# Layer 0 of a four-layer graph network: the two operands of the edge-counting matmuls change places

## The reference

```python
m = relu(node_feat[src] + edge_feat)                      # 200000 x 32
neigh = segment_sum(m, dst, num_segments=N)               # by destination
x = layernorm(x + (1.0 + eps[0]) * node_feat + neigh)
```

## Time and profile before

| | us |
|---|---|
| median of 3 runs | 11489.69 |
| lowest and highest of them | 11487.98, 11491.17 |
| the profiled execution, first to last instruction (its span; the profile gives no other time of it) | 11493.4 |
| layer 0's loop in it, first pick to last | 169.4 to 1386.3 |

### The profile page before, as it was taken

The page is one execution under the profiler, slowest core; times in us unless marked ns, Lnnn a source line. Parts: engine busy times, 40 slices in busy tenths (PEclk is TensorE's granted clock), DMA queues, the critical chain, the costliest instruction groups (busy, mean ns, idle before and its releaser), DMA issues. The chain is left out here.

```text
span 11493.4 us, 152259 instructions
## 1 busy us (share of the span) xinstructions
PE 10456.3 (91%) x55143; PEld 9959.3 (87%) x55143; DVE 8163.2 (71%) x11101; ACT 6663.2 (58%) x6595; POOL 8130.8 (71%) x8260
## 2 busy tenths in 40 slices
PE   4999759996999999998999799979999799979997
PEld 4999758885999999998999799979999799979996
DVE  5767658886888888886666566656666566656665
ACT  2444335555888888884555455545555455535554
POOL 3777777775666666664777677767777677767776
PEclk9999979997999999999999899989999899989998
DMA  6333234434333333332333233323333233323332
GB/s 215 118 120 106 80 74 98 100 98 126 90 84 85 88 85 87 86 85 76 107 107 108 76 111 110 109 85 100 111 107 107 78 107 110 111 75 107 110 107 78
DMA packets 657979, 1157.05 MB, mean 101 GB/s; under 512 B 187206, under 2 KB 446019, under 8 KB 638787
## 3 DMA queue, kind: packets, MB, share of 16 engines
q1 hardware_dynamic: 353303, 819.43, 21.5%
q0 software_dynamic: 288992, 294.48, 12.7%
q10 hardware_dynamic: 15384, 40.39, 1.1%
HBM read 776.79 MB, written 419.18 MB: 104 GB/s over the span
## 5 line engine op out<-in xcount | busy, mean ns | idle before, releaser
L2240 PE MATMUL ps<-qs,oh 128*128 128x416 f32 (+1 forms) x26880 | 5291.9, 352 | 129.6 <-ACT oh L2330 59.9
L2119 POOL DMA_INDIRECT l3g<-TQ,srcs x4480 | 4306.1, 961 | 1524.6 <-issue 1079.8
L2240 PEld LDWEIGHTS ps<-qs,oh 128*128 128x128 f32 x26880 | 4867.5, 188 | 400.2 <-DVE l3g L2411 214.2
L2411 DVE TENSOR_REDUCE l3g<-ps 128x32 f32<-128x416 f32 x3360 | 1894.5, 583 | 1563.2 <-PE ps L2240 1563.0
L2330 ACT CAST oh<-nd 128x1536 fp32r<-128x1536 bf16 x1120 | 1654.9, 1478 | 1692.3 <-DVE nd L2407 1692.3
L1989 PE MATMUL ps<-l2mm,l2oh 128*128 128x408 f32 (+1 forms) x12544 | 2391.3, 352 | 24.4 <-DVE l2mm L2061 24.4
L1989 PEld LDWEIGHTS ps<-l2mm,l2oh 128*128 128x128 f32 x12544 | 2333.5, 189 | 65.0 <-DVE l2mm L2061 25.2
L1973 POOL DMA_INDIRECT l2g<-Y,place x1568 | 1598.2, 1019 | 816.6 <-DVE l2mm L2061 400.0
L2061 DVE TENSOR_TENSOR l2mm<-l2hl,psv 128x1768 fp32r<-128x1768 f32 x784 | 1532.2, 1992 | 262.6 <-PE ps L1989 258.7
L2004 ACT ACTIVATE l2oh<-l2far,l2one 128x512 fp32r<-128x512 f16 x1568 | 1135.2, 724 | 294.0 <-PE ps L1989 291.5
L1151 POOL DMA_INDIRECT l0g<-T,srcs x896 | 968.7, 1081 | 420.0 <-issue 224.2
(11 more groups left out here) (394 smaller groups left out, 7303.8 us busy)
## 6 DMA issues: line engine op xcount, KB each, us to landing
W<-l3o SPq DMA_DIRECT2D x140, 1792.0 KB
mneg<-KG SPq DMA_DIRECT2D x280, 384.0 KB
l3km<-KG SPq DMA_DIRECT2D x280, 360.0 KB
l3g<-TQ,srcs POOLq DMA_INDIRECT x4480
l3t<-AT SPq DMA_DIRECT2D x140, 448.0 KB, 3.9
W<-l1o SPq DMA_DIRECT2D x28, 952.0 KB, 4.1
l0e<-U_a SPq DMA_DIRECT2D x28, 896.0 KB, 4.6
S<-RX SPq DMA_DIRECT2D x49, 512.0 KB
```

The source lines that it names most:

```text
L2119: e.indirect_dma_start(G3[s][:, j, :], None, TQ, bass.IndirectOffsetOnAxis(ap=srcs[:, c * C + j:c * C + j + 1], axis=0)).then_inc(z3[f"g{s ...
L2240: x_ = e.matmul(ps[k % 3][:, 0:32 * n], OH[k // SB][:, g, 128 * (k % SB):128 * (k % SB) + 128], QS[:, p, 32 * n0:32 * (n0 + n)], start=g = ...
L2411: e.tensor_reduce(G3[r // KP % 3][:, C - KP + r % KP, :], ps[r % KP % 3][:, 0:32 * PH].rearrange("p (h f) -> p f h", f=32), AXX, ALU.max). ...
```

## The change

The counting matmuls take the 49 one-hots of the high part as weights and stream the 128 of the low part, so the counts build up turned, as [49, 128], in `ps[3]`. The opening matmul of zeros has its operands swapped in the same way. At the end VectorE copies the counts to a new tile `cntT` [64, 128], TensorE transposes that into `ps[1][:, 0:49]`, and VectorE copies the result to `cnt` as before; a new semaphore `back` orders the three.

```diff
+        cntT = sb(l0, "cntT", [64, 128])
...
-        hi = Named(sem, "hist", "split oh used cnted base first zero")
+        hi = Named(sem, "hist", "split oh used cnted base first zero back")
...
         def count_dst_v(e, vc):
             e.wait_ge(hi["used"], NG)
             z = vc.up(e.memset(BD.ex[:, :], 0.0).then_inc(vec, 1))
-            e.tensor_copy(cnt[:, :], ps[3][:, 0:NC]).then_inc(hi["cnted"], 1)
+            e.tensor_copy(cntT[0:NC, :], ps[3][0:NC, 0:128]).then_inc(hi["back"], 1)
+            e.wait_ge(hi["back"], 2)
+            e.tensor_copy(cnt[:, :], ps[1][:, 0:NC]).then_inc(hi["cnted"], 1)
...
                 for j in range(H):
-                    x_ = e.matmul(ps[3][:, 0:NC], BD.AL[x % 2][:, :, j], BD.AH[x % 2][:, :, j],
+                    x_ = e.matmul(ps[3][0:NC, 0:128], BD.AH[x % 2][:, :, j], BD.AL[x % 2][:, :, j],
                                   start=False, stop=False, skip_group_check=True)
...
-            e.matmul(ps[3][:, 0:NC], ident[:, :], zer[:, 0:NC], start=True, stop=False, skip_group_check=True)
+            e.matmul(ps[3][0:NC, 0:128], zer[:, 0:NC], ident[:, :], start=True, stop=False, skip_group_check=True)
...
+            e.wait_ge(hi["back"], 1)
+            e.transpose(ps[1][:, 0:NC], cntT[0:NC, :], ident[0:NC, 0:NC]).then_inc(hi["back"], 1)
             e.wait_ge(hi["cnted"], 2)
             e.matmul(ps[0][:, 0:1], slt[:, :], BD.ex[:, NC:NC + 1], start=True, stop=True).then_inc(hi["base"], 1)
```

## The result

| | us |
|---|---|
| kernel before, median of 4 runs | 11488.83 (11486.91 to 11491.17) |
| changed kernel, median of 4 runs | 11736.39 (11732.73 to 11737.59) |
| ratio, 95% interval | 1.0215 (1.02 to 1.0229) |
| forecast, range | 11635, 11560 to 11710 |

The change costs 248 us, 2.15%. The sign was forecast and the size was not: +145 us were expected, and the result lies 26 us above the range. The profiled execution's span is 11731.0 us.

The account below looks back on a forecast made before the run. GpSimd was taken to pace layer 0 at 44 us a chunk, and TensorE after the change at 48.8. Loop +151 and tail -7 gave +144, kept as +145 on 11489.7: 11635 us, range 11560 to 11710.

Parts of the forecast that it names:

- What bounds the kernel: Layer 0: GpSimd's gathers set the pace from about the fifth chunk, 44 us a chunk; TensorE has some 3 us slack.
- Step 1: Counting matmuls: streaming 128 strided columns for 49 takes 240 ns each instead of 93; the 49-column load hides.
- ScalarE's strided copy: Argument that strided reads are slow: copying across rows takes 2.0 ns an element, casting adjacent elements 0.95.
- The lowest bound: Counting matmul of 128 columns at the picks' 0.46 ns a column, if the stride is free: 59 ns.
- Step 2: Counting group: 3.36 us for 1.30, next pick's 0.08 us load wait goes; net +1.98 a group, +7.9 a chunk.
- Rival C: TensorE: counting groups bring the lower clock, 1.5 us each; 170 us more at every group, 34 at one in five; 0.05.
- step 3: Layer 0's other engines: gathers get some 5 us slack, VectorE and ScalarE stay below 48.8; TensorE bounds, 3 us stalls vanish.
- step 5: Layer 0's tail: last add follows the last reduction within about 1 us instead of 8.1; -7 us.
- step 6: Counts turned at the end: copy, transpose, copy take 0.8 to 1.1 us inside VectorE's 1.3 us idle; 0.
- rival A: Counting matmul costs 59 to 122 ns, GpSimd still sets the pace; no change, 11485 to 11492 us; 0.14.
- rival B: Counting matmul costs 160 to 200 ns, part of the 93 being fixed; at 180, 11542 us; 0.06.
- rival D: Faster, needing GpSimd's gathers to be quicker because TensorE is; 0.01.

Follow-up runs that it names:

- b_plus7_3: Kernel before with 7 more counting matmuls in each group, into PSUM columns that nothing reads; 11504.65 against 11491.43 us, ratio 1.0011.
- a_pairs_3: Changed kernel with one-hots laid out as [7, columns, 2], neighbouring columns 4 bytes apart instead of 28; 11482.52 against 11491.43 us, ratio 0.9991.
- a_wide: Changed kernel with weights 128 columns wide, 49 one-hots and 79 zeros; ratio 1.0099 on a chip with held-up gathers (kernel before 14238 us).
- a_split: Changed kernel with each counting group done in two halves of 7, behind a pick and behind the next; 11704.8 us, ratio 1.0189.
- b_pairs: Kernel before, operands not swapped, with one-hot columns 4 bytes apart instead of 28; 14266.51 us, ratio 1.001, on a chip with held-up gathers.
- a_wide_split_3: Changed kernel with weights zero-padded to 128 columns and each group in two halves of 7; 11649.18 against 11491.43 us, ratio 1.0135.

## Why the prediction was wrong, point by point

**What bounds the kernel** was read rightly. GpSimd paces layer 0 before (`b_plus7_3`: 13 us of 73 show; `a_pairs_3`: a group shorter by 0.38 us brings nothing that can be told from zero), and TensorE after. The turn comes a chunk later than said, after six chunks.

**Step 1, the price of a streamed column**, was right: 240 ns taken, 232 measured, 1.8 ns a column. The load of 49 hides as said. The 49 columns took 168 ns to load, 89 above the fixed 79 where I had 93. `a_pairs` shows the cause. Of the arguments, the one from ScalarE's strided copy was an analogy that no run tested. The lowest bound, 59 ns at the picks' rate, was slightly too high: `a_pairs` streams 128 adjacent columns in 57. The cheaper column is worth -0.45 us a chunk, -13 us.

**Step 2 failed in its joints.** It said that after a group the next pick's wait for its own load "goes", +0 instead of 0.08 us. It doesn't go; it grows. In the changed kernel a group with its joints costs 3.40 us plus 0.10 on the pick before and 0.10 on the pick behind (medians 1.558 to 1.577 and 1.564 to 1.597 us against 1.473 for the others on average), 3.60 in all, of which 14 x 232 = 3.25 are streams: **0.35 us of joints a group**, 1.4 a chunk, about 39 us in all. The first wide load isn't fetched ahead: the loads of the changed kernel's timeline stand still for 0.40 us between the last narrow and the first wide one. In `a_wide`, second below, no such pause stands between the group's loads and the pick's.

```profile
647.34 3.00 PEld L1231 LDWEIGHTS ps<-bdAL,bdAH 128*49 128x49 bf16 x14 [0.25 <-DVE bdAL L616]
650.74 0.86 PEld L1222 LDWEIGHTS ps<-qs,l0oh 128*128 128x128 f32 x5 [0.40 <-issue]
```

```profile
305.74 2.98 PEld L1233 LDWEIGHTS ps<-bdAL,wr 128*128 128x128 bf16 x14 [0.16 <-issue]
308.81 1.24 PEld L1224 LDWEIGHTS ps<-qs,l0oh 128*128 128x128 f32 x4
```

That it is the width of the weights follows from `a_wide` (0.3 us less a group) and from `a_split` (twice the joints: 51.1 us a chunk, 1.3 more than the 49.8 that a chunk of 51.3 with one low stretch has without it).

**Rival C, the clock, happened** and had 0.05. Its price was right, 1.5 us each time, and its mechanism too (a stretch in which columns come at a quarter of the usual rate), but I held it unlikely and put it at nothing in the sum. 47 stretches came, behind 4 groups in 10: 47 x 1.5 = 71 us. I had only rows in which an idle engine brought the low clock, and took slow streaming for work.

The sum for the loop: forecast 1368, less 13 for the columns, plus 39 for the joints, plus 71 for the clock = 1465 us; measured 1467. The median missed by 101 us; the loop of the profiled execution missed by 99, and these terms make 97 of them; steps 3, 5 and 6 stand. The range ended 75 us above the forecast: it had room for either of the two terms, not for both.

**Rivals A, B and D** are out: A and B by the 232 ns, D by the slower result. A's own consequence, that a cheap stream would gain nothing, is what `a_pairs_3` shows.

No version is measurably faster than the kernel before. The cheapest counting (`b_pairs`, 0.40 us a group) frees 3.6 us of TensorE a chunk where GpSimd is the bound, and its total on a chip that isn't held up was not measured; to turn that into time, columns would have to move from gathers to picks, which wasn't tried.

## What to carry to other kernels

Before a matmul's operands are swapped to stream the longer one, look at how far apart its columns lie: here 28 bytes made a column 1.8 ns instead of 0.45, and the layout mattered more to TensorE than the order of the operands. Cost a group of odd matmuls with its joints, and ask of every stretch of slow streaming what the clock will do behind it; two halves between other work were cheaper than one whole. First of all find who sets the pace: while GpSimd did, 2.6 us more of TensorE a chunk cost 13 us of 73, and 1.1 us less brought nothing measurable.

## What the runs showed of the hardware that was not expected

- Streaming at 1.8 ns a column for 3.4 us lowered the granted clock to 1.2 GHz behind it, in 47 of 112 cases, with no idle time before; in halves of 7 matmuls never, in 224 cases (`a_split`, 1.8 us each) and 224 (`a_wide_split_3`, about 1.6 us).
- A change between 49 and 128 columns of weights costs about 0.35 us for the two joints together, of which 0.3 go when the narrow weights are padded with zeros to 128 (`a_wide`).
- Loading 49 columns of bf16 weights took longer than loading 128: 168 ns against 142 at 28 bytes between columns (`after`, `before`), 103 against 98 at 4 bytes (`a_pairs_3`, `b_pairs`).
- Spacings of TensorE held across chips (93 to 95 ns for 49 columns, 232 to 235 for 128) while the same kernel before took 11487 us on some chips and 14003 to 14248 us on others, with GpSimd's gathers mostly 1.25 us apart but some 3 us. What held them up was not looked into.
